# A state-space stage with its states summed on TensorE, its input products on GpSimd, and its rows copied by ScalarE

## The reference, cut to what matters

```
dbc = x @ Wx
dt = softplus(dbc[..., :DT_RANK] @ Wdt + bdt)
Bm = dbc[..., DT_RANK:DT_RANK + D_STATE]
Cm = dbc[..., DT_RANK + D_STATE:]
dA = exp(dt[..., None] * A)
dBx = dt[..., None] * Bm[:, :, None, :] * x[..., None]
def step(hc, ins):                 # over the 512 steps
    hc = dA_t * hc + dBx_t
    y = einsum('bdn,bn->bd', hc, C_t)
y = (y + Dp * x) * silu(z)
return y @ Wout
```

## Time and profile before

| | us |
|---|---|
| median of 3 runs | 5366.92 (5365.64 to 5392.56) |
| profiled execution | 5376.71 |
| its span, first to last instruction | 5374.9 |
| state-space stage within the span, from the first recurrence | 1577 to 1990 |

### The profile page before, as it was taken

The page is one execution under the profiler, slowest core; times in us unless marked ns, Lnnn a source line. Parts: engine busy times, 40 slices in busy tenths (PEclk is TensorE's granted clock), DMA queues, the critical chain, the costliest instruction groups (busy, mean ns, idle before and its releaser), DMA issues. The chain is left out here.

```text
span 5374.9 us, 89012 instructions
## 1 busy us (share of the span) xinstructions
PE 4317.4 (80%) x27516; PEld 3073.2 (57%) x27516; DVE 3450.0 (64%) x6519; ACT 2656.3 (49%) x7533; POOL 2357.6 (44%) x1611
## 2 busy tenths in 40 slices
PE   6888897888854437888888888888888888687788
PEld 4666564666521105666666666666666666355566
DVE  5555123555569987887787787877877886344412
ACT  3333343444233425666666666666666665234333
POOL 3443001333015556665566666655665664133300
PEclk8888998999965559999999999999999998567799
DMA  0000000000000001111111111111111110000000
GB/s 19 2 1 2 36 0 21 2 1 2 14 3 0 0 26 49 35 30 31 48 29 30 49 30 30 55 30 30 50 29 30 29 30 23 19 1 0 0 32 8
DMA packets 47561, 114.91 MB, mean 21 GB/s; under 512 B 16240, under 2 KB 22792, under 8 KB 46472
## 3 DMA queue, kind: packets, MB, share of 16 engines
q1 hardware_dynamic: 47112, 109.33, 7.5%
HBM read 34.85 MB, written 2.10 MB: 7 GB/s over the span
## 5 line engine op out<-in xcount | busy, mean ns | idle before, releaser
L2049 ACT ACTIVATE l2f_p<-ps,l2f_negmax 128x96 f32<-128x96 f32 x1536 | 503.6, 340 | 401.9 <-DVE l2f_negmax L1891 392.3
L1528 PE MATMUL ps<-l2f_wqkv,l2f_xsT 128*128 (+1 forms) x1152 | 580.4, 628 | 73.2 <-ACT l2f_xsT L2009 56.5
L1425 POOL TENSOR_TENSOR l2f_rn<-l2f_ss,neghalf 128x16 f32<-128x16 f32 x192 | 558.4, 2908 | 165.8 <-DVE l2f_ss L1859 165.8
L1431 POOL TENSOR_TENSOR l2f_cosd<-xnT,l2f_rot 128x1024 f32<-128x1024 f32 x192 | 521.6, 2717 | 149.8 <-DVE xnT L1866 149.8
L1875 DVE TENSOR_TENSOR xn<-xnT,l2f_rot 128x512 f32<-128x512 f32 x384 | 577.6, 1545 | 10.1
L1472 POOL TENSOR_TENSOR l2f_p<-l2f_p,l2f_rinv 128x384 f32<-128x384 f32 x384 | 317.6, 827 | 594.9 <-DVE l2f_rinv L1900 594.8
L1584 PE MATMUL ps<-l2f_pT,l2f_vw 96*128 96x128 f32 x3072 | 434.9, 286 | 15.4 <-DVE l2f_pT L1909 13.9
L1584 PEld LDWEIGHTS ps<-l2f_pT,l2f_vw 96*128 96x128 f32 x3072 | 391.5, 198 | 61.4 <-issue 51.9
L1558 PEld LDWEIGHTS ps<-l2f_kT,l2f_qz 128*128 128x128 f32 x3072 | 403.3, 196 | 11.8 <-issue 7.7
L1558 PE MATMUL ps<-l2f_kT,l2f_qz 128*128 128x96 f32 x3072 | 402.6, 275 | 0.0
L2065 ACT COPY l2f_oT<-ps 64x256 f32<-64x256 f32 x768 | 282.1, 367 | 174.9 <-PE ps L1584 160.9
(11 more groups left out here) (352 smaller groups left out, 9856.8 us busy)
## 6 DMA issues: line engine op xcount, KB each, us to landing
l2f_vw<-l2f_vt SPq DMA_DIRECT2D x96, 384.0 KB, 4.1
l2f_vw<-l2f_vt SPq DMA_DIRECT2D x96, 256.0 KB, 3.6
l2f_wqkv<-L_ffn_Wqkv_dram SPq DMA_DIRECT2D x18, 512.0 KB
l2f_vw<-l2f_vt SPq DMA_DIRECT2D x72, 128.0 KB, 2.3
l0f_w<-L_w_dram SPq DMA_DIRECT2D x2, 2304.0 KB
l3f_w<-L_w_dram SPq DMA_DIRECT2D x2, 2048.0 KB
l2f_wo<-L_ffn_Wo_dram SPq DMA_DIRECT2D x6, 512.0 KB
l2f_w<-L_ffn_W_dram SPq DMA_DIRECT2D x6, 344.0 KB
```

The source lines that it names most:

```text
L1425: nc.gpsimd.tensor_tensor(rn[:, k], ss[:, k], g.neghalf[:, 0:HEADS], ALU.pow).then_inc(rn_ready[k], 1)
L1431: nc.gpsimd.tensor_tensor(cosd[:, k].rearrange("p (h d) -> p h d", d=DH), nrm[:, k].rearrange("p (h d) -> p h d", d=DH), rot[:, it.odd, k, ...
L1528: ins = nc.tensor.matmul(g.ps[:, 2 * (k % 2) + hf], xsT[:, WINDOW + t * P:WINDOW + (t + 1) * P], wqkv[:, bass.ds(weight_slot(it), 1), k * ...
L2049: ins = nc.scalar.activation(p[:, n % 2, c], g.ps[:, 4, c * KW:(c + 1) * KW], ACT.Exp, bias=negmax[:, col:col + 1], accum_out=rowsum[:, co ...
```

## The change

The running sum `ysum` in SBUF and GpSimd's additions go. TensorE's new `add_up` multiplies `hc` by the identity in fp32 and accumulates the 16 states of a scan in PSUM bank 5; `yg` reads that bank. VectorE's `input_part` goes: ScalarE's new `copy_row` copies B's row from PSUM to one of three `row` buffers in SBUF, and GpSimd multiplies it by `dtx` into one of three `dBx` buffers (`slot`). In ScalarE's loop copy n - 3 stands behind decay n and ahead of the threaded steps of that n; copies 13 to 15 stand behind the loop, copy 0 of the next scan between its decays 1 and 2. In TensorE's loop `add_up` of state n - 1 stands ahead of `spread` of state n + 2, and the B product now waits for the copy of the row two before it, not for the input product.

```
-                for n in range(N):
-                    pool.wait_ge(hc_ready, at(b, u, N, n + 1))
-                    if n == 0:
-                        pool.wait_ge(y_ready, at(b, u, 1, 0))
-                        nc.gpsimd.tensor_tensor(ysum[:], hc[:, n % 2], zero[:].broadcast_to([P, SEQ]),
-                                                ALU.add).then_inc(y_added, 1)
-                    else:
-                        pool.wait_ge(y_added, at(b, u, N, n))
-                        nc.gpsimd.tensor_tensor(ysum[:], ysum[:], hc[:, n % 2], ALU.add).then_inc(y_added, 1)
+                pool.wait_ge(dtx_ready, at(b, u, 1, 1))
+                for n in range(N):
+                    pool.wait_ge(row_ready, at(b, u, N, n + 1))
+                    pool.wait_ge(hs_ready, at(b, u, N, n - 2))
+                    nc.gpsimd.tensor_tensor(dBx[:, slot(b, u, n)], row[:, slot(b, u, n)], dtx[:, u],
+                                            ALU.mult).then_inc(dBx_ready, 1)
...
+            def add_up(b, u, n):
+                if n == 0:
+                    pe.wait_ge(y_ready, at(b, u, 1, 0))
+                pe.wait_ge(hc_ready, at(b, u, N, n + 1))
+                nc.tensor.matmul(g.ps[:, 5], g.ident[:], hc[:, n % 2],
+                                 start=(n == 0), stop=(n == N - 1)).then_inc(y_added, 1)
...
-                    pe.wait_ge(dBx_ready, at(b, u, N, n - 1))
+                    pe.wait_ge(row_ready, at(b, u, N, n - 1))
                     nc.tensor.matmul(g.ps[:, n % 2], sel[:, n], split[:, u],
                                      start=True, stop=True).then_inc(b_ready, 1)
...
                 for n in range(N):
+                    if n:
+                        add_up(b, u, n - 1)
                     spread(b, u, n + 2)
                     if ahead and n in (1, 5, 8):
                         {1: inputs, 5: low_rank, 8: time_steps}[n](*ahead)
                 if ahead:
                     spread(*ahead, 0)
+                add_up(b, u, N - 1)
+                if ahead:
                     spread(*ahead, 1)
...
-            def input_part(b, u, n):
-                dve.wait_ge(b_ready, at(b, u, N, n + 1))
-                nc.vector.tensor_tensor(dBx[:, n % 2], g.ps[:, n % 2], dtx[:, u], ALU.mult).then_inc(dBx_ready, 1)
...
-                    if n + 1 < N:
-                        input_part(b, u, n + 1)
                     dve.wait_ge(c_ready, at(b, u, N, n + 1))
                     dve.wait_ge(hs_ready, at(b, u, N, n + 1))
                     dve.wait_ge(y_added, at(b, u, N, n - 1))
...
-                ch.done(nc.vector.scalar_tensor_tensor(yg[:], xc[:, u], par["vec"][:, u, 2:3], ysum[:],
+                ch.done(nc.vector.scalar_tensor_tensor(yg[:], xc[:, u], par["vec"][:, u, 2:3], g.ps[:, 5],
                                                        ALU.mult, ALU.add))
...
+            def copy_row(b, u, n):
+                act.wait_ge(b_ready, at(b, u, N, n + 1))
+                act.wait_ge(dBx_ready, at(b, u, N, n - 2))
+                nc.scalar.copy(row[:, slot(b, u, n)], g.ps[:, n % 2]).then_inc(row_ready, 1)
+
             def first_decays(b, u):
                 act.wait_ge(dt_ready, at(b, u, 1, 1))
-                for n in range(FIRST):
-                    decay(b, u, n)
+                decay(b, u, 0)
+                decay(b, u, 1)
+                copy_row(b, u, 0)
+                decay(b, u, 2)
+                decay(b, u, 3)
 
             def scan(b, u, ahead):
                 for n in range(FIRST, N):
                     decay(b, u, n)
+                    copy_row(b, u, n - 3)
                     if ahead and n in (5, 7, 10, 12):
                         {5: copy_input, 7: gated, 10: copy_low_rank, 12: soft}[n](*ahead)
+                for n in range(N - 3, N):
+                    copy_row(b, u, n)
```

More of the change, by code:

```diff
@@ L860, in l2_attn_stage @@
         dA = sb("dA", [P, DA, SEQ])
-        ysum = sb("ysum", [P, SEQ])
-        zero = sb("zero", [P, 1])
-        dBx = sb("dBx", [P, 2, SEQ])
+        row = sb("row", [P, 3, SEQ])
+        dBx = sb("dBx", [P, 3, SEQ])
         hs = sb("hs", [P, 2, SEQ])
@@ L870, in l2_attn_stage @@
         pre = once("pre")
-        zero_ready = once("zero_ready")
         var_ready = once("var_ready")
@@ L890, in l2_attn_stage @@
         dt_ready = sem("dt_ready")
+        dtx_ready = sem("dtx_ready")
+        row_ready = sem("row_ready")
         split_ready = sem("split_ready")
@@ L910, in at, with slot @@
             return CREDIT + u * per + k + b * 2 * per
+        def slot(b, u, n):
+            return (n + u) % 3
         def both_ways(eng, scan, end=lambda: None):
@@ L1087, in time_steps @@
                 dve.wait_ge(dt_ready, at(b, u, 1, 1))
-                ch.done(nc.vector.tensor_tensor(dtx[:, u], dt[:, u], xc[:, u], ALU.mult))
-            def input_part(b, u, n):
-                dve.wait_ge(b_ready, at(b, u, N, n + 1))
-                nc.vector.tensor_tensor(dBx[:, n % 2], g.ps[:, n % 2], dtx[:, u], ALU.mult).then_inc(dBx_ready, 1)
+                nc.vector.tensor_tensor(dtx[:, u], dt[:, u], xc[:, u], ALU.mult).then_inc(dtx_ready, 1)
             def scan(b, u, ahead):
@@ L1098, in scan @@
                     dve.wait_ge(dA_ready, at(b, u, N, n + 1))
-                    nc.vector.tensor_tensor_scan(hs[:, n % 2, way], dA[:, n % DA, way], dBx[:, n % 2, way], 0.0,
+                    nc.vector.tensor_tensor_scan(hs[:, n % 2, way], dA[:, n % DA, way], dBx[:, slot(b, u, n), way], 0.0,
                                                  ALU.mult, ALU.add).then_inc(hs_ready, 1)
-                    if n + 1 < N:
-                        input_part(b, u, n + 1)
                     dve.wait_ge(c_ready, at(b, u, N, n + 1))
@@ L1108, in scan @@
                         {4: convolve, 9: split_rows, 12: time_steps}[n](*ahead)
-                if ahead:
-                    input_part(*ahead, 0)
                 dve.wait_ge(y_added, at(b, u, N, N))
-                ch.done(nc.vector.scalar_tensor_tensor(yg[:], xc[:, u], par["vec"][:, u, 2:3], ysum[:],
+                ch.done(nc.vector.scalar_tensor_tensor(yg[:], xc[:, u], par["vec"][:, u, 2:3], g.ps[:, 5],
                                                        ALU.mult, ALU.add))
```

4 lines of the change are left out of this document (removed).

## The result

The changed kernel takes 5511.24 us (median of 4 runs, 5504.84 to 5515.58) against 5373.45 us before (median of 4 runs, 5365.64 to 5392.56): 1.0257 times as long, 95% interval 1.0233 to 1.0281. Its profiled execution took 5511.58 us, its span is 5510.0 us where that of before was 5374.9: 135.1 us more.

A forecast was written before the change was run, and what follows sets the result against it. VectorE was taken as the bound (48.66 of 52 us a scan). ScalarE waits +81, Gelu +11 and stage start +2 made +94 us: 5471 against the profiled 5376.7, 5461 against the median; range 5405 to 5505.

The forecast's parts named there:

- The four waits: Copies 3, 5, 8 and 10 stand behind ScalarE's waits in seven prefetching scans: 11.6 us a scan, +81 us.
- The step: One state on VectorE: recurrence and GpSimd product alternate through the port lock, 2.32 us against 2.31; bounds 2.14 to 2.56.
- gated: ScalarE's wait at n=7 for VectorE's convolution delays recurrence 5: taken as +3.5 us a prefetching scan.
- The tail from release to recurrence: After each ScalarE release: decay 0.61, copy 0.59, product 1.26, two handovers under 0.1; 2.6 us to the next recurrence.
- copy_input and Gelu: ScalarE's wait for projections at n=5, +3.5 us a prefetching scan; Gelu ahead of copy 1, +3.6 three times.
- low_rank: ScalarE's copy at n=10 delays recurrence 8: +1.3 us a prefetching scan, including +0.15 for a row behind an fp32 sum.
- soft: ScalarE's wait at n=12 for the time-step product delays recurrence 10: +3.3 us a prefetching scan.
- (a): TensorE at the high clock for most of the stage: -28 to -45 us, 5416 to 5433; chance 0.14.
- (b): TensorE stays at the low clock and its 2.6 us a step binds: +38 us, 5499; chance 0.08.
- (c): GpSimd product and recurrence overlap, step 1.90 us: -52 us, 5409; chance 0.08 for slower, shared with (e).
- (d): GpSimd keeps three products ahead, so ScalarE's waits cost nothing: 22 or 52 us gained, 5315 to 5345; chance 0.05.
- (e): Step stays 2.31 us and half of the 11.6 us waits is hidden: about 5415; chance 0.08 shared with (c).

The follow-up runs named there:

- recurrence_first: The changed kernel with GpSimd's products 2, 4, 6, 9 and 11 held until the recurrence of the state before is done; 5496.26 us, 1.0229 times before.
- sums_ahead: The changed kernel with TensorE's fp32 sum and B row put ahead of the threaded projections at states 1, 5 and 8; 5538.24 us (1 run).
- sums_alone: The changed kernel with input products back on VectorE and no ScalarE copies, sums still on TensorE; 5386.93 us, 1.0029 times before.
- last_sum_only: The changed kernel with only state 15 summed on TensorE, one fp32 sum per scan in place of sixteen; 5496.37 us, 1.0231 times before.
- write_only: The changed kernel with GpSimd writing a constant into the product buffer instead of multiplying two SBUF rows, waits kept; 5421.09 us (1 run).
- both_orders: The changed kernel with ScalarE's copies ahead of its waits and TensorE's sums and B products ahead of the threaded products; 5400.81 us, 1.0048 times before.

## Why the prediction was right in its mechanism and short in its size

The prediction was 5461 us, range 5405 to 5505; 5511 lies 6 us above the range. Point by point:

- *What bounds, and the waits.* Right. The four waits appear at states 3, 5, 8 and 10 and the fifth at state 1 behind the Gelu, all released by GpSimd behind a ScalarE copy. Of the 122.7 us for which VectorE waited for GpSimd, the four are 102.5 and those at state 1 are 13.8. They are 3.3 to 5.3 us each at states 3, 5 and 10, as foretold, but only 1.4 at state 8. Taking their cause away takes 94.6 us from the stage. The end of a scan, taken at 0, is -1.2 over seven.
- *The step, taken as unchanged at 2.32.* Right on balance only. States 10 to 15 cost 1.8 us over seven scans, but in them recurrence 10 and the one behind `time_steps` run long (by 7.4 and 6.5 us over the seven), and VectorE's time steps no longer meet a GpSimd sum (4.02 us from recurrence 12 to 13 in most scans, where it was 4.91). In the last scan the 15 steps take 37.4 us, 2.50 each (2.14 to 3.02), against 2.31 before, so the step is nearer to the upper end of 2.56 than to what was taken.
- *gated, +3.5.* Measured 24.1 / 7 = 3.4, and 25.2 / 7 = 3.6 by taking it away. The tail from release to recurrence, 2.6, measured 2.57 and 2.58.
- *Start, +2.* Measured 1.8.
- *copy_input and Gelu, low_rank, soft.* These three terms of the sum were mis-sized: 35.3, 9.1 and 23.1 us were taken, 44.8, 17.9 and 30.3 measured, 25.5 us too little together. The step that failed is the handover at the end of the tail, "two handovers of under 0.1: 2.6 us to the next recurrence". I ended the tail where the recurrence starts and let it run 1.22 us. In the trace GpSimd's next product takes the port at that moment, and the recurrence takes 2.27 us. The `hc` that comes out late is what TensorE's next C row waits for, and the threaded projections stand behind that row (1749.66 to 1750.94 in the timeline), so the loss reaches the next wait. Recurrences 1, 3, 5 and 8, which stand ahead of these three waits, ran 27.1 us longer over the seven scans than at 1.215 us each, against the 25.5 missing. `recurrence_first` bears it out: with these at 1.22 us the three terms are 39.0, 10.5 and 18.8, 68.3 in sum where I had 67.5. That the sums meet so closely is partly luck, for the single terms are 3.7 and 1.4 us over and 4.3 under, and the edit also holds up states of its own and takes `hc`'s wait for TensorE from 14.2 to 3.1 us. The gated term alone came out exact; VectorE's own convolution releases it, and no row or product of TensorE lies between state 4 and that release.
- *low_rank, "+0.15 for the row product that now stands behind an fp32 sum".* Also too small: copy 8 waited 0.44 us for its row, and `hc` of state 7 2.46 for the sum of state 5. This second wait I had not seen at all. It is covered in the changed kernel, where VectorE waits another 1.40 us for the product behind it (and `sums_ahead`, which takes it away, gains nothing). In `sums_alone`, where no copy covers it, the same sum holds up the input product of state 8, and the column is 11.0 us.
- *The last scan, 0.* Measured 2.3: the 15 steps are 2.8 longer, the end 0.5 shorter.
- *Everything outside the stage, 0.* 12.0 us in the fourth layer, as above; without it the profiled execution, 5511.6, would lie inside the range. The sum of the terms was 94 against 5376.7, 5471; by the same terms it measured 121.7 (119.9 and 1.8), and 13.4 lie beside them.

The rivals. (a), TensorE at the high clock: it did rise, 0.57 to 0.69 in the third scan, but nowhere near a steady 1.00, and the gain was not there to be seen in the sum; only `last_sum_only`, 19.4 us longer with one sum in place of sixteen, lets it be seen. (b), its 2.6 us a step binding, gave 5499, nearest to what came, and is wrong: VectorE waits 14.2 us for TensorE at `hc` and 122.7 for GpSimd. (c), no exclusion: wrong, 2.27 us against the 1.214 of `write_only`. (d), the copies not late: wrong as the kernel stands, and with them as early as in `both_orders` it is no gain, 1.0048 times before; a step of 2.55 us against 2.31 in the last scan says that GpSimd's product cost more there than VectorE saved. (e), whose sum is 5417 and not 5415, is wrong: VectorE's 16 input products a scan are gone and the step did not get shorter, but the waits were not hidden by half.

## What to carry over

An instruction moved to another engine inherits that engine's queue: list every wait that stands ahead of it there, and ask what was buffered across that wait before and isn't now; here the stretches with the five such waits made 117.1 of the 119.9 us. When two engines share a port, price the late one as losing it, with a whole instruction of the other's ahead of it, and follow that delay into the next chain. A change in two halves is worth timing as halves: here the accumulator gains 0.3% once its order is right, and the products took the kernel from 1.0029 (`sums_alone`) to 1.0257 times before.

## What the runs showed of the hardware

- With added TensorE work in the stage its granted clock was higher: 0.71 with the sixteen fp32 sums and 0.54 with one, and the stage with more work was 19.4 us shorter. With the products on VectorE it was 0.56 without the sums (before) and 0.79 with them (`sums_alone`). A sum, two matmuls in the trace, took 1.02 us at 1756.21, where the granted clock was 1.00, and 1.91 at 1738.38, where it was 0.50.
- A VectorE instruction that had been waiting for GpSimd's product 4.64 us was overtaken by GpSimd's next one: 2.27 us for the recurrence and not 1.22. Of the 128 recurrences 44 took over 1.9 us, 27 of the 28 behind the four waits among them.
- GpSimd writing 128x512 fp32 constants (0.52 us) beside the recurrence cost it nothing (1.214 us, at most 1.226).
- The fourth layer's attention, the same code in all kernels, took 486.4 to 540.6 us, longer with a lower granted clock (0.70 to 0.60).
